# Two interleaved layer norms taken one at a time in the first stage of an attention-and-experts block

## What is computed

```python
xn = _layernorm(x, axis=-1)                        # first norm, eps 1e-5
x = x + attention(xn, ...) + experts(xn, ...)

# attention: a second norm of xn, then projections
mu = jnp.mean(x, -1, keepdims=True)
var = jnp.var(x, -1, keepdims=True)
xn = (x - mu) * jax.lax.rsqrt(var + LN_EPS) * gamma + beta
h = jnp.einsum('bsd,fd->bsf', xn, W1)              # input of the pairwise part
qkv = jnp.einsum('bsd,ed->bse', xn, Wqkv) + bqkv
# experts: router logits of the first norm
logits = jnp.einsum('td,de->te', x_flat, router)
```

## Time and profile before

| | |
|---|---|
| median of 3 executions | 1670.21 us (1669.36 to 1673.53) |
| the profiled execution's own time | 1673.36 us |
| span of its instructions | 1671.6 us |
| busy, of the span | PE 97%, VectorE (DVE) 91%, ScalarE (ACT) 87%, GpSimd (POOL) 64% |
| first stage | from the start to about 97 us |
| mean granted TensorE clock | 0.999 |

### The profile page before, as it was taken

How to read it: one execution, slowest core, us unless ns; L and a number is a source line. 1 busy time by engine, 2 the same in 40 slices (tenths; PEclk the granted TensorE clock), 3 DMA queues, 4 the chain that set the end, 5 groups by cost and what they waited for, 6 DMA issues and landing times.

```text
span 1671.6 us, 32654 instructions
## 1 busy us (share of the span) xinstructions
PE 1622.3 (97%) x9092; PEld 707.6 (42%) x9092; DVE 1524.5 (91%) x4301; ACT 1448.7 (87%) x2676; POOL 1075.1 (64%) x1009
## 2 busy tenths in 40 slices
PE   7989999999999999999999999999999999999998
PEld 6742222222222222222222222222222799988887
DVE  6877789999999999999999999999998698868777
ACT  4679999999999999999999999999999778844342
POOL 3203467777777777777777777676776644366644
PEclk9999999999999999999999999999999999999999
DMA  4512211212122121212122111111131465434233
GB/s 159 197 60 73 102 45 49 65 50 63 53 63 64 46 68 47 66 48 66 52 61 65 49 50 47 42 49 41 44 128 32 135 186 181 153 121 126 82 109 113
DMA packets 78331, 135.89 MB, mean 81 GB/s; under 512 B 22336, under 2 KB 43712, under 8 KB 78272
## 3 DMA queue, kind: packets, MB, share of 16 engines
q0 software_dynamic: 31744, 69.27, 15.2%
q1 hardware_dynamic: 46528, 65.92, 11.7%
HBM read 91.04 MB, written 39.85 MB: 78 GB/s over the span
## 4 chain that ended last, share of the span: by engine, by line
DVE 54%; PE 28%; issue 7%; ACT 3%; DVEq 1%; DMA 0%; ACTq 0%
DVE arena L1377 29%; PE ps L893 17%; PE ps L853 8%; DVE arena L1445 4%; DVE arena L1435 3%; DVE arena L1415 3%; DVE idx L1402 3%; DVE smax L1426 2%; PE ps L864 2%; DVE arena L1401 2%; DVE top L1395 2%; DVE arena L1420 1%; DVE arena L1430 1%; ACT arena L1062 1%; PE ps L910 1%
## 5 line engine op out<-in xcount | busy, mean ns | idle before, releaser
L684 POOL DMA_INDIRECT arena<-kv_rows,gidx x800 | 859.4, 1074 | 358.1 <-issue 220.8
L853 PE MATMUL ps<-arena,w2t 128*64 128x512 f32 x4096 | 946.3, 600 | 10.0 <-DVE arena L1377 4.6
L1377 DVE TENSOR_SCALAR arena<-arena 128x256 f32<-128x256 f32 x2464 | 770.0, 371 | 20.7 <-PE ps L853 18.4
L1062 ACT ACTIVATE arena<-arena 128x256 f32<-128x256 f32 x1632 | 728.3, 550 | 12.5 <-DVE arena L1367 12.5
L1075 ACT ACTIVATE arena<-ps,b 128x1024 f32<-128x1024 f32 x512 | 589.6, 1152 | 4.1 <-PE ps L853 3.9
L853 PEld LDWEIGHTS ps<-arena,w2t 128*64 128x64 f32 x4096 | 268.3, 136 | 676.7 <-issue 514.8
L864 PE MATMUL ps<-arena,w3win 128*32 128x512 f32 x2048 | 272.7, 605 | 8.2 <-DVE arena L1387 8.2
L652 POOL DMA_INDIRECT slot_inputs<-xstage,istage x64 | 70.2, 1096 | 97.6 <-issue 62.4
L864 PEld LDWEIGHTS ps<-arena,w3win 128*32 128x32 f32 x2048 | 40.3, 108 | 216.2 <-issue 155.9
L1445 DVE TENSOR_TENSOR arena<-arena 128x1152 f32<-128x1152 f32 (+4 forms) x160 | 100.8, 630 | 0.3
L762 POOL DMA_INDIRECT arena<-slot_outputs,slot_get x64 | 69.0, 1078 | 22.0 <-issue 15.5
(11 more groups left out here) (150 smaller groups left out, 1925.4 us busy)
## 6 DMA issues: line engine op xcount, KB each, us to landing
arena<-kv_rows,gidx POOLq DMA_INDIRECT x800
slot_inputs<-arena SPq DMA_DIRECT2D x16, 640.0 KB, 3.9
arena<-slot_inputs SPq DMA_DIRECT2D x40, 256.0 KB, 3.6
slot_outputs<-arena SPq DMA_DIRECT2D x40, 256.0 KB, 2.3
arena<-in_L_attn_x_dram SPq DMA_DIRECT2D x16, 256.0 KB, 3.0
xstage<-arena SPq DMA_DIRECT2D x16, 256.0 KB
xn_rows<-arena SPq DMA_DIRECT2D x16, 256.0 KB
arena<-in_L_attn_x_dram SPq DMA_DIRECT2D x8, 512.0 KB, 4.1
```

The lines of the kernel that those rows point to most:

```text
L684: pool.indirect_dma_start(out=kvg[:, h, r, :], out_offset=None, in_=kv_dram, in_offset=bass.IndirectOffsetOnAxis(ap=gidx[:, h, r:r + 1], a ...
L853: last = nc.tensor.matmul(ps_l2(s)[v * G2:(v + 1) * G2, u, :], w2t[:, :], r1[:, s % R1, 4 * u + 2 * v:4 * u + 2 * v + 2, :], start=True, s ...
L1062: last = nc.scalar.activation(r1[:, s % R1, k, :], hneg_now, ACT.Relu, bias=hb_now[:, at:at + 1])
L1377: row = nc.vector.tensor_scalar(r1[:, s % R1, k, :], hneg_now, hb_now[:, at:at + 1], 0.0, ALU.add, ALU.max)
```

## The change

In the loop pass and in the written-out pass 0, the one call of `statistics` for both norms becomes two calls, one per norm. Norm 0's `bn_stats`, `bn_aggr` and `veps` all stand ahead of norm 1's. The instructions are the same, and so are their number, sizes and waits; GpSimd's list is untouched.

```diff
             def both_layernorms(b):
                 dve.wait_ge(x_loaded, b * 16 + 32)
-                statistics((b + 1, 0), (b, 1))
+                statistics((b + 1, 0))
+                statistics((b, 1))
                 normalize(b + 1, 0)
                 normalize(b, 1)
                 save_logits(b)
```

## The result

The changed kernel takes 1678.17 us in the median of 6 executions (1676.91 to 1681.81), the kernel before 1672.38 in 6 beside them (1669.36 to 1673.92). The ratio is 1.0039 with a 95% interval of 1.0028 to 1.0049: 6.5 us slower, 4.7 to 8.2 (the medians lie 5.8 apart). Two later series gave 1.0045 (1.0031 to 1.0059) and 1.0037 (1.0025 to 1.0049). The profiled execution took 1677.37 us with a span of 1675.6. The forecast was 1673.7. That was wrong. 1678.17 is inside its range of 1670.0 to 1678.5, but the forecast was +3.5 us, a change that can't be told from none, and the kernel is slower clear of the interval, by nearly twice that much. The range reached so far for another reason, a slow sequencer, which did not come true.

What follows compares the result with a forecast made beforehand. The first stage was taken to turn on one chain: statistics, GpSimd's roots, normalising, copies. Passes 3 to 14 at +0.29 us each gave +3.5 on the median 1670.21, so 1673.7 us, range 1670.0 to 1678.5.

Steps and rivals of the forecast that it cites:

- slow sequencer: Rival, slower: register work between the two norms' statistics takes 0.7 us, 8.7 us more in all, 1678.9; chance 0.17.
- The gain: VectorE's 0.58 us wait ahead of norm 0's normalising goes; GpSimd's first root ends at 2.39 instead of about 3.04.
- Norm 0's chain: From a loop pass's first `bn_stats` to norm 0's `veps`, its statistics taken alone: 1.45 us.
- d: Time from the start of norm 0's `veps` to norm 1's first `bn_stats`, for register and wait instructions: 0.30 us.
- Norm 1's chain: Norm 1's statistics, root and normalising end at 4.61 + d into the pass, which grows by 0.29 us.
- TensorE's clock: Rival, slower: loop passes with more TensorE pause run matmuls at 1.2 GHz, each costing 3.5 us more; chance 0.02.
- The clock behind the stage: Pairwise part's first matmuls, partly at 1.2 GHz, cost 1.6 us now; 1.6 went to either side of the range.
- The rival of free dependent steps: Rival, faster: dependent VectorE steps cost nothing, chain some 0.6 shorter, gain 0.50 a pass, 6.0 in all, 1664.2; chance 0.05.

## Why the prediction was wrong

**The gain, right.** The wait of 0.58 ahead of the first normalising went, the first root ran alone and early.

**Norm 0's chain, right.** 1.45 us to `veps` as batch 15 had shown: 46.00 - 44.55.

**d, right.** 0.30 forecast, 0.31 measured, and the run with the moved waits shows that it is what I took it for. The estimate scaled the instructions' own lengths by 1.9, from one place, the loop entry. With one instruction of 80 ns left it was 0.14, or 1.75 times its length, so the hit is not mere luck, but the factor is no constant.

**Norm 1's chain, the smaller miss: short by 0.05.** I put the end of the normalising at 4.91 into the pass; it is 47.97 + 1.54 - 44.55 = 4.96. The step from norm 1's `bn_stats` to its `veps` took 1.47 instead of 1.45 inside the loop, and its root 0.71 instead of 0.69. With d, a pass grew by 0.35 instead of 0.29, 4.2 us instead of 3.5 over 12 passes; pass 2 cost 0.1 and not 0.03. This term alone would have left the forecast standing at 1674.5.

**TensorE's clock: the step that failed.** The sum +3.5 has no term for a fall of the clock within the loop. The prediction named it as a rival ("TensorE's clock falls in the loop"), gave it 0.02 and priced a pass with a fall at 3.5 us, by pass 1, in which all matmuls were slow. It argued that TensorE would still be busy 4.64 of 5.43 us, as if that were close enough to 4.64 of 5.14. The profiles say otherwise: all three of the changed kernel, both with the VectorE delay, the one with moved waits and the one with two transposes have one to three falls before 100 us, while none of the five with passes of 5.16 or less, and none of the three with four transposes a pass, has one inside the loop. The price was wrong too: a fall lasts 3.4 us, catches the two projections, and costs 1.26 here, 1.23 to 1.48 in all. In the stage of the profiled execution the sum of 3.5 was short by 3.3: 2.5 of it are two falls of the clock, 0.8 the chain. The 6.8 of the stage agrees with the measured 6.5 (4.7 to 8.2). How much of the program's time is due to the falls stays open: the run with the late transposes had none, a stage only 4.4 longer than the kernel before profiled again, and still 6.0 us (3.8 to 8.2) in time.

**The clock behind the stage, no change.** The 1.6 set aside to either side was not needed: the first 32 matmuls of the pairwise part took 8.53 us after the change, 8.78 before.

**The rival of free dependent steps, refuted.** The gaps of 0.15 to 0.16 are there, 48 of them in 12 passes, and regrouping an equal number of instructions was not free. The rule of the Trainium skill against which I had weighed the row ("VectorE: DVE Perf Modes", section on the DRAIN you can't avoid) says that the semaphore between VectorE instructions costs nothing extra, which the page measured on eight tensor_copy. What I drew from it for these short dependent instructions, each behind a wait instruction of its own, the measurement refutes; what the same instructions would take without the semaphores no run here shows. In the same place I took 4.64 us, TensorE's busy time, as the floor of a pass; the version with all `bn_stats` in front ran into a floor at 5.02, that of TensorE and ScalarE waiting for each other in turn.

## What to carry to other kernels

Where two chains of short dependent instructions are interleaved on one engine, each fills the gaps of the other; before pulling one forward, add up the gaps that open in it, the sequencer's work that loses its cover, and the later start of the other chain. Keep long independent instructions together in front and let only the short chains follow one another: that gave the early root without the cost. And when a loop gets longer while TensorE's work stays the same, count TensorE's clock as a term of its own, with its price taken per fall from the matmuls that it would catch.

## What was not expected of the hardware

A lengthening of the pass by 0.21 us, from 5.14 to 5.35, with the same matmuls in it, went along with two falls of the granted clock from 1.00 to 0.5 in twelve passes, each 3.4 us long, in both profiles of that kernel; with passes of 5.16 and below none of five profiles had one. And d, 0.31 us, stood between two VectorE instructions that do not wait for each other at all. Between them ran three register and wait instructions, 160 ns by their own length, and 0.14 us remained when two of them were moved away.
